# Attention step on TensorE: the row-maximum block split by head pairs, and the last unit's sums shared between GpSimd and VectorE

## The reference

```python
def _L0_attn_b_ref(x, Wq1, Wq2, Wk, Wv, Wlam, Wo):
    H = 16; B, T, D = x.shape; d = D // H          # d = 32
    q = jnp.concatenate([q1, q2], axis=1)          # 32 query heads of 32
    scores = jnp.einsum('bhqd,bhkd->bhqk', q, k2) * scale
    scores = jnp.where(causal, scores, jnp.finfo(scores.dtype).min)
    p = jax.nn.softmax(scores, axis=-1)
    y = jnp.einsum('bhqk,bhkd->bhqd', p, v2)
    y = y1 - lam * y2
    return y.transpose(0, 2, 1, 3).reshape(B, T, D) @ Wo
```

## Time and profile before

| | us |
|---|---|
| median of the 3 runs (2129.99 to 2134.12) | 2130.41 |
| the profiled execution's own time | 2131.86 |
| its span, first to last instruction | 2130.0 |
| attention, from 975 to 1764 of the span | about 790 |

### The profile page before, as it was taken

One profiled execution on the slowest core, in us unless ns is written; L12 is line 12 of the kernel. 1 busy time (PEld: TensorE's weight loads), 2 busy tenths in 40 slices (PEclk: granted clock), 3 DMA queues, 4 the chain that ended last, 5 costly groups with the idle time before them and its releaser, 6 DMA issues.

```text
span 2130.0 us, 29410 instructions
## 1 busy us (share of the span) xinstructions
PE 2035.2 (96%) x11824; PEld 902.1 (42%) x11824; DVE 1271.8 (60%) x1838; ACT 855.3 (40%) x1304; POOL 888.4 (42%) x457
## 2 busy tenths in 40 slices
PE   7998999999999999999999999999999879899999
PEld 3444444444444445343434334343433323444444
DVE  5868687647746634455555555555556623775634
ACT  4434353334434322434443434344344442443431
POOL 3766585600000001666666666766766681000000
PEclk9999999999999999999999999999999999999999
DMA  7111110300000011000001010000000101000001
GB/s 232 35 30 35 30 36 30 129 15 1 1 1 1 1 48 26 1 16 14 18 11 21 5 27 1 16 16 16 2 11 6 61 30 40 1 1 20 21 1 40
DMA packets 68999, 55.53 MB, mean 26 GB/s; under 512 B 36800, under 2 KB 55232, under 8 KB 68608
## 3 DMA queue, kind: packets, MB, share of 16 engines
q1 hardware_dynamic: 61952, 41.07, 6.6%
q10 hardware_dynamic: 6912, 12.59, 2.0%
HBM read 43.02 MB, written 10.62 MB: 25 GB/s over the span
## 4 chain that ended last, share of the span: by engine, by line
PE 53%; DVE 4%; ACT 3%; POOL 3%; issue 1%; DVEq 0%; ACTq 0%; POOLq 0%
PE psum L116 9%; PE psum L1151 8%; PE psum L1239 8%; PE psum L1300 6%; PE psum L1283 5%; PE psum L140 5%; PE psum L1189 3%; POOL b_totals L1524 2%; PE psum L1279 2%; PE psum L1245 2%; PE psum L1257 2%; DVE b_maxima L1587 2%; PE psum L1270 1%; PE psum L1197 1%; ACT b_probs L1446 1%
## 5 line engine op out<-in xcount | busy, mean ns | idle before, releaser
L1524 POOL TENSOR_TENSOR b_totals<-b_totals,b_probs 128x2048 f32<-128x2048 f32 (+3 forms) x160 | 515.4, 3221 | 311.1 <-ACT b_probs L1446 304.9
L1587 DVE TENSOR_REDUCE b_maxima<-psum 128x2 f32<-128x1024 f32 (+3 forms) x384 | 350.6, 954 | 392.4 <-PE psum L1245 232.9
L1446 ACT ACTIVATE b_probs<-psum 128x1024 f32<-128x1024 f32 (+3 forms) x320 | 228.6, 765 | 256.4 <-PE psum L1283 233.1
L435 PE MATMUL psum<-hT,a_win 128*128 128x512 f32 x640 | 293.1, 601 | 0.8 <-ACT hT L555 0.8
L116 PE MATMUL psum<-hT,b_early 128*128 128x512 f16 x1024 | 228.2, 383 | 5.2 <-DVE b_middle L202 5.2
L116 PE MATMUL psum<-hT,W 128*128 128x512 f16 x1024 | 226.4, 381 | 3.9 <-DVE a_win L202 3.9
L435 PEld LDWEIGHTS psum<-hT,a_win 128*128 128x128 f32 x640 | 120.4, 193 | 130.8 <-issue 129.5
L116 PEld LDWEIGHTS psum<-hT,b_early 128*128 128x128 bf16 x1024 | 100.2, 98 | 131.5 <-issue 10.6
L116 PEld LDWEIGHTS psum<-hT,W 128*128 128x128 bf16 x1024 | 100.4, 98 | 126.5 <-DVE a_win L202 7.6
L1501 POOL MEMSET b_mask<- 128x128 f32 x1 | 0.2, 204 | 356.8 <-POOLq L267 356.8
L1634 DVE RECIPROCAL b_down<-b_down 128x128 f32<-128x128 f32 x128 | 111.9, 918 | 40.7 <-ACT b_down L1424 40.7
(11 more groups left out here) (225 smaller groups left out, 3285.0 us busy)
## 6 DMA issues: line engine op xcount, KB each, us to landing
a_parts<-in_w_guT ACTq DMA_DIRECT2D x32, 256.0 KB, 2.8
ternary<-W SPq DMA_DIRECT2D x1, 6144.0 KB, 18.1
a_win<-in_w_inT SPq DMA_DIRECT2D x20, 256.0 KB, 7.2
a_parts<-in_w_pT ACTq DMA_DIRECT2D x16, 256.0 KB, 2.6
b_down<-lam_rows SPq DMA_DIRECT2D x32, 128.0 KB, 2.7
b_early<-ternary SPq DMA_DIRECT2D x8, 512.0 KB, 7.8
out<-x SPq DMA_DIRECT2D x16, 256.0 KB, 2.2
x<-in_x SPq DMA_DIRECT2D x3, 1024.0 KB, 7.3
```

The costliest lines, as they stand in the source:

```text
L435: last = pe.matmul(ring(s, j), win[:, at:at + P], core["hT"][:, (i * KT + k) * BLK:(i * KT + k + 1) * BLK], start=(k == 0), stop=(k == KT ...
L1446: act.activation(held(u, s)[:, 2 * a:2 * a + 2, off:BLK], pair_banks(("score", u, s, a))[:, :, off:BLK], ACT.Exp, scale=SCALE).then_inc(ex ...
L1524: pool.tensor_tensor(acc, acc, held(u, s)[:, :, off:BLK], ALU.add).then_inc(summed, 1)
L1587: dve.tensor_reduce(maxima[u % 2][:, :].rearrange("p (h q c) -> p h q c", h=HPT, q=QT)[:, 2 * a:2 * a + 2, qt, kc], pair_banks(("row", u, ...
```

## The change

Three edits.

1. The row block is cut in two. `half_row(..., 0)` with heads 0 and 1 stays where the block was; `half_row(..., 1)` with heads 2 and 3 moves to the end of the step, behind fills and output. Its masks (`row_masks`) and the masks of the next step's scores (`score_masks`) are issued in front of it, so that it runs straight into the bias and score matmuls of the next step. `PAIR_USES` follows: the output now takes its pair between the two halves.
2. In the last unit GpSimd sums heads 0 and 1 only, and VectorE sums heads 2 and 3 (`share_sum`, semaphore `shared`).
3. The last `den`, its copy and its reciprocals go behind the first group of matmuls of the feed-forward.

```diff
         if row_in(_u, _i):
-            PAIR_USES += [("row", *row_in(_u, _i), a) for a in range(2)]
+            PAIR_USES.append(("row", *row_in(_u, _i), 0))
         if out_in(_u, _i):
             PAIR_USES.append(("out", *out_in(_u, _i), 0))
+        if row_in(_u, _i):
+            PAIR_USES.append(("row", *row_in(_u, _i), 1))
...
+            def half_row(u, n, a, masks_first=False):
+                qt, kc = ROWS[n]
...
+                first = diagonal and masks_first
+                for j in range(2):
+                    at = 2 * a + j
+                    last = pe.matmul(to[:, j, 0:width], strip(qT[w][r % 2], at, qt * P, (qt + 1) * P),
+                                     strip(kT[w][r % 2], at, kc * BLK, hi), start=not first,
+                                     stop=first or not diagonal, skip_group_check=first)
...
                     if row_in(u, i):
-                        row(*row_in(u, i))
+                        half_row(*row_in(u, i), 0)
...
                     if out_in(u, i):
                         output(*out_in(u, i))
+                    if row_in(u, i):
+                        row_masks(*row_in(u, i))
+                    if u * NS + i + 1 < UNITS * NS:
+                        score_masks(*divmod(u * NS + i + 1, NS))
+                    if row_in(u, i):
+                        half_row(*row_in(u, i), 1, masks_first=True)
             weigh(UNITS - 1, NS - 1)
-            for job in EPILOGUE:
-                fill_all(job)
...
-                acc = heads(total[(u * CQ + c) % 2])[:, :, off:BLK]
-                pool.tensor_tensor(acc, acc, held(u, s)[:, :, off:BLK], ALU.add).then_inc(summed, 1)
+                own = slice(0, 2 if u == UNITS - 1 else HPT)
+                acc = heads(total[(u * CQ + c) % 2])[:, own, off:BLK]
+                pool.tensor_tensor(acc, acc, held(u, s)[:, own, off:BLK], ALU.add).then_inc(summed, 1)
...
+            def share_sum(u, s):
+                c, kt = STEPS[s]
+                off, g, n = step_width(s), u * NS + s, summed_by(u, s) - EARLIER_SUMS
+                dve.wait_ge(exped, 2 * g + 2)
...
+                acc = heads(total[(u * CQ + c) % 2])[:, 2:HPT, off:BLK]
+                dve.tensor_tensor(acc, acc, held(u, s)[:, 2:HPT, off:BLK], ALU.add).then_inc(shared, 1)
```

More of the change, by code:

```diff
@@ L1248, in row, with row_masks, score_masks @@
                             last.then_inc(row_done, 1)
+            def half_row(u, n, a, masks_first=False):
+                qt, kc = ROWS[n]
+                r, w = divmod(u, 2)
+                if n == 0 and a == 0:
+                    pe.wait_ge(fill_copied, FREED_BY_ACT[NTH[("q", r, w, CQ - 1)]])
+                hi = min((kc + 1) * BLK, (qt + 1) * P)
+                width, diagonal = hi - kc * BLK, kc == qt // TPB
+                to = pair_banks(("row", u, n, a)) if masks_first else take_pair(("row", u, n, a))
+                first = diagonal and masks_first
[4 more added lines that the diff above has]
+                                     stop=first or not diagonal, skip_group_check=first)
+                if diagonal and not masks_first:
+                    for j in range(2):
+                        last = pe.matmul(to[:, j, width - P:width], later_key[:, :], ident_b[:, :],
+                                         start=False, stop=True)
+                last.then_inc(row_done, 1)
+            def row_masks(u, n):
+                qt, kc = ROWS[n]
+                width, diagonal = min(BLK, (qt + 1) * P - kc * BLK), kc == qt // TPB
+                to = take_pair(("row", u, n, 1))
+                if diagonal:
+                    for j in range(2):
+                        pe.matmul(to[:, j, width - P:width], later_key[:, :], ident_b[:, :], start=True, stop=True)
+            def score_masks(u, s):
+                c, kt = STEPS[s]
+                off = step_width(s)
+                if kt >= TPB * c:
+                    for a in range(2):
+                        to = take_pair(("score", u, s, a))
+                        for j in range(2):
+                            pe.matmul(to[:, j, off:off + P], ident_b[:, :], later_key[:, :], start=True, stop=True)
             def output(r, two):
@@ L1363, in hook @@
                 def hook(m):
+                    if i == 0 and m == 0:
+                        for job in EPILOGUE:
+                            fill_all(job)
                     if i == 0 and 3 <= m < 3 + QT:
@@ L1696, in _ @@
                     split(("neg", 0))
-                row(*divmod(n, NR))
+                for a in range(2):
+                    half_row(*divmod(n, NR), a)
             for u in range(UNITS):
@@ L1716, in _ @@
                         early_stats(i)
-            for half in range(2):
-                invert(UNITS - 1, 1, half)
+                    if u == UNITS - 1 and STEPS[i][1]:
+                        share_sum(u, i)
             dve.wait_ge(out_added, len(OUTS))
@@ L1754, in hook @@
                 def hook(m):
+                    if i == 0 and m == 0:
+                        for part in range(2):
+                            invert(UNITS - 1, 1, part)
                     if i == 0 and 4 <= m < 4 + QT:
```

41 lines of the change are left out of this document (24 added, 17 removed).

## The result

The changed kernel takes 2271.14 us (median of four runs, 2268.88 to 2277.68) against 2132.21 us for the kernel before in the same session (four runs). The ratio is 1.0657, with a 95% interval of 1.0637 to 1.0677: slower by 139 us. The forecast was 2249 us, range 2215 to 2285, main case 2230 to 2265. The profiled execution took 2269.26 us, its span 2267.2; that is 137.4 us more than the profiled execution of before, where the sum said 119.

What follows compares the result with a forecast made beforehand. TensorE, busy 96% of the span, was taken to bound the kernel. Terms 120 + 29 - 28 - 4 + 4 + 9 - 11 = +119 us on the profiled 2131.86 gave 2251, median 2249, range 2215 to 2285.

Steps and rivals of the forecast that it cites:

- main case: Whole kernel: a median of 2230 to 2265 us, given 62%; the half row of heads 2 and 3 is paid in full.
- Half rows, +120: TensorE, 162 steps: two heads cost as much as four, 0.84 us per 512 columns plus 0.11 start; bounds +102 to +146.
- Strict order: Rival, 6%: no matmul starts before those ahead in program order; bias of heads 2 and 3 waits 1.16 us, not 0.96; 2280.
- The half row hidden: Rival, 3%: the half row of heads 2 and 3 costs almost nothing, so its +120 and +9 vanish; median 2120 us.
- Output waits, +29: Second pair of next-step score masks waits 1.2 us for VectorE's output addition, 24 of 28 outputs in the regular stretch: +29 us.
- What goes away, -28 and -4: Row blocks stop waiting for same-step exponentials, -28 us; the half row covers one score block's row-maximum wait per unit, -4.
- Maxima, +4: First half row waits for the previous step's second-half maximum, 0.3 us in step 3 of each of 13 units: +4 us.
- rival of late maxima: Rival, 10%: the next half row waits 0.3 us for maxima in most steps, not one of twelve; +35 us, 2285.
- Units 13 and 14, +9: 16 steps after fills end: 11 pay for half rows (9), 5 pay nothing; outputs +5, fewer exponential waits -5; +9 us.
- The last unit, -11: Shared sums, GpSimd and VectorE taking turns, save about 7 us, later denominators 4: -11 us, between -8 and -16.

Runs made afterwards that it cites:

- e6: The changed kernel with the half row at the end of the step (heads 2 and 3) cut to 128 columns in every step: 2186.12 us, ratio 1.025.
- e5: The changed kernel with the row block whole again in its old place, the next scores' masks still issued at the step's end: 2125.67 us, ratio 0.996.
- e10: The changed kernel with VectorE's addition of each output cut from 512 to 32 columns, all orders unchanged: 2246.42 us, ratio 1.0526.
- e3: The changed kernel with the next scores' masks back inside the score block, behind the half row of heads 2 and 3: 2236.94 us, ratio 1.0501.
- e1: The kernel before with edits 2 and 3 alone, its row blocks left whole: 2121.71 us, ratio 0.995.
- e2: The changed kernel without edits 2 and 3, so only the rows are split: 2281.48 us, ratio 1.0697 to the kernel before.

## Why the prediction was right, and where its sum was off

The direction, the mechanism and the range held. The point was 22 us low against the median of 2271.14, and the main case, up to 2265, was missed by 6 us. The table sets the forecast's terms beside what the two profiles show. In units 0 to 12 each block is measured from its start to the start of the next one. The forecast's terms for 162 steps are taken for the 156 steps of these units; the other six belong to unit 13. (Unit 0 of the attention begins at 834 us; the 975 and the 930 us ahead of the prediction and in it are points inside the attention.)

| us | forecast | measured |
|---|---|---|
| units 0 to 12: half rows and scores, against the scores alone | 115 - 4 | 110.3 |
| masks of the scores, with the output waits | 29 | 34.3 |
| first half rows, against whole row blocks with their waits | -27 | -32.3 |
| time ahead of the first half rows (maxima) | 4 | 9.6 |
| masks of row blocks, outputs, fills | 0 | 3.9 |
| units 13 and 14 | 12 | 21.2 |
| unit 15 and all behind it | -11 | -8.4 |
| ahead of unit 0 | 0 | -1.3 |
| sum | 118 | 137.3 |

The measured sum is the 137.2 us between the two spans, to rounding. Several terms missed by 5 us or more, and in both directions; that the sum came as near as 18 us is in part luck.

**Half rows, +120.** Right. In the profile, half row and scores to the weighing take, at 512 columns of scores, 2.13, 1.92, 1.71 and 1.49 us for half rows of 512, 384, 256 and 128 columns, against 1.20 for the scores alone. That is 0.085 + 0.85 for each 512 columns: 117 x 0.853 + 156 x 0.083 = 113 in units 0 to 12, less 4 for the scores' own waits, which went. The row that the forecast rests on, two heads no cheaper than four, is borne out by 1.05 us for a half row alone, and by e6.

**Strict order, rival, 6%.** Refuted: with 512 columns on both sides the bias of heads 2 and 3 follows the half row by 0.97 us (1416.39 to 1417.36), the figure of the main case and not 1.16. It is 0.96 behind every half row of 512 columns in units 0 to 12, whatever the width of the scores. The half row's second pass starts at 1416.93, behind the start, at 1416.64, of score matmuls that stand after it in the program.

**The half row hidden, rival, 3%.** Refuted by e5 and e6.

**Output waits, +29.** Right, a little short: the pair comes 1.43 us behind the first instead of 0.11, 1.3 each and not 1.2, so 32 for 24. e10 shows the price directly.

**What goes away, -28 and -4.** The waits for exponentials are gone. In the kernel before, row blocks of units 0 to 12 have 7.9 us of marked idle time ahead of matmuls; 5.4 of it name an exponential and 2.5 VectorE's addition of an output, which the prediction, from one case, had read as ended by then. Shorter waits are not marked: taken together the row blocks last 28 to 30 us longer than the shortest of their width would, the size forecast. The few us left of the 32.3 are the half block itself, 1.05 instead of 1.07 to 1.11 us.

**Maxima, +4.** This term was too small. I had put one wait of 0.3 us into each unit, in step 3. There the first half row of 128 columns starts 0.50 us later behind its weighing than the row block of before did. Step 10, also 128 columns wide, loses 0.16, step 2 0.07, and in step 11 a new wait for a maximum, in every second unit, stands against a wait for an output that the other units no longer have. The rival of late maxima in most steps (+35) did not come.

**Units 13 and 14, +9.** This is the step that failed in size. The +9 is for the 16 steps from where the fills end; the first six steps of unit 13 were counted in the other terms, with 4.5 x 0.84 + 6 x 0.11 = 4.4 less 1, so that the whole stretch was forecast at about +12. Measured 133.9 - 112.7 = +21. Most of the 9 between them is the clock, for which the prediction has no term: the granted clock fell to 0.92 there, from 0.97, (1 - 0.92) x 133.9 = 10.7 us lost at most against (1 - 0.97) x 112.7 = 3.4, which is up to 7. The waits of the masks for maxima, 7.7 us, are no cause: they were 6.4 before. Of the five steps that were charged nothing ("in 5 nothing separates the halves or the wait is longer than the half row") three did cost nothing, one 0.8 us, and one ran at half clock (6.45 us before, 8.52 after). What e3 adds is that the charged steps need not have paid. Three steps of unit 13, at full clock, grow from weighing to weighing from 4.61, 4.60 and 4.59 us to 5.32, 5.53 and 5.48: TensorE waits for a maximum first, as before, and the half row comes on top. In e3, where the half row stands ahead of that wait, they take 4.60, 4.60 and 4.55.

**The last unit, -11.** By the medians 10.5 us (e1) and 10.3 (e2), in the two profiles 8.4. The last weighing stands 38.3 us behind the first of unit 15 before and 32.5 after, 5.8 less where the sums were forecast to give 7; the feed-forward starts 0.9 us behind it instead of 5.4; and what follows is 2.0 us longer, where 1.0 was allowed for the denominators. The sums alternate as forecast, by 2.93 us against 1.23. The Trainium skill, "SBUF — State Buffer", section "Who interferes with whom", says that a VectorE instruction with two SBUF inputs and a GpSimd instruction that reads SBUF contend for one port pair, and that it is locked exclusively. The trace agrees, by the 2.93 us and by GpSimd's 3.40 where 2.36 is usual. The Trainium skill, "TensorE: Matmul & The Clock Gate", section "Part 3: Packing small matmuls — row/col tiling", says that matmuls start and end in program order. For starts this does not hold in this trace, by the 1416.93 above; the ends of matmuls are modelled in these rows and show nothing.

## What to carry to other kernels

Where row strips of the array work side by side, count blocks and not heads: here a block with half of the strips costs what the full one costs (1.05 against 1.11 us), and splitting it can pay only if something else runs on the idle strips and nothing waits behind the half, which no run here reached. When an order of buffers is changed, write down for each use which read it now follows and what stands between them; a wait moved from a wide matmul's back to its front cost 1.3 us each time. Where two engines take turns on a memory, as here, try giving the whole job to the faster one before sharing it: that was worth 5.8 us.

## What was not expected of the hardware

In units 13 and 14 TensorE's granted clock falls to half for some stretches, and what runs there takes twice as long. Timeline of PE in the changed kernel, unit 14 (a pair of masks that waited, then weighing and output), and in the second fence two stretches there, with the columns of the stretches above:

```profile
1843.28 0.28 PE L1293 MATMUL psum<-b_later_key,b_ident_b 128*128 128x128 bf16 x2 [1.11 <-DVE b_maxima L1636]
...
1846.49 1.94 PE L1338 MATMUL psum<-b_probs,b_middle 128*32 128x512 f32 x8
...
1850.55 3.73 PE L1302 MATMUL psum<-b_wo,b_down 128*128 128x512 f32 x4
```

```profile
1838.00:1843.30 5.30, 4.19 (x31) 1.41 (x32) 4.29 (x5) 1.94 (x2) 4.23 (x2) 1.00 1.01 328
1843.80:1853.80 10.00, 10.00 (x34) 3.00 (x27) 2.45 (x2) 1.62 (x2) 6.67 (x3) 0.52 0.01 2
```

The engine is busy 4.19 of 5.30 us at full clock and then 10.00 of 10.00 at a mean of 0.52, which is the lower of the two levels, 1.2 GHz, nearly throughout. The output takes 3.73 us there and 1.88 above, and its whole step 10.99 us, where e3 has 6.38. In the regular stretch, with TensorE busy 96% of the time even after the change, the clock is 1.00. In units 13 and 14 of the kernel before and of the changed one the low clock began at the end of a wait of 1.1 to 2.5 us or about 1 us behind it, but of the 24 output waits in units 0 to 12 only one was followed by it (the 0.99 of the stretch from 1386 to 1523.9). So whether waits bring it about, and what decides it, stays open: e10 has shorter waits than the changed kernel and a lower clock in units 13 and 14 (0.87), e3 with few waits has 0.96, and no run changed the waits there alone.
